# The last pair of a split-precision Strassen product: one product moved to the end, in two quarters

## The reference, cut to what matters

```python
# x: (8, 256, 1024) float32, 2048 tokens
base = einsum('btd,od->bto', x, W)                 # W: (1024, 1024)
logits = einsum('btd,ed->bte', x, Wr) + bias       # 8 experts, 5.0 added to the language's own
gates = softmax of the top 2 logits, 0 elsewhere
h = einsum('btd,erd->bter', x, A)                  # rank 16
y = base + 2.0 * einsum('bter,bte,eor->bto', h, gates, B)
dots = softmax(y @ centroids.T / 0.1)              # 64 clusters
hits = dots > 0.01
query_sel, cluster_sel = any(hits, axis=1), any(hits, axis=0)
dense = y @ weight.T + ffn_bias                    # (1024, 1024)
out = x + where(query_sel[:, None] & cluster_sel[assignments][None, :], dense, 0)
```

## Time and profile before

| | us |
|---|---|
| median of 3 runs | 349.85 (349.26 to 349.99) |
| the profiled execution | 350.19 |
| its span, from the first to the last instruction | 348.1 |
| TensorE busy / weight loads | 337.4 / 296.7 |
| VectorE busy | 254.1 |
| ScalarE busy | 134.0 |
| granted TensorE clock, mean | 0.994 |

### The profile page before, as it was taken

One profiled execution on the slowest core, in us unless ns is written; L12 is line 12 of the kernel. 1 busy time (PEld: TensorE's weight loads), 2 busy tenths in 40 slices (PEclk: granted clock), 3 DMA queues, 4 the chain that ended last, 5 costly groups with the idle time before them and its releaser, 6 DMA issues.

```text
span 348.1 us, 4828 instructions
## 1 busy us (share of the span) xinstructions
PE 337.4 (97%) x1892; PEld 296.7 (85%) x1892; DVE 254.1 (73%) x439; ACT 134.0 (39%) x215; POOL 1.0 (0%) x9
## 2 busy tenths in 40 slices
PE   6799999999999999999999999999999999999993
PEld 6588888999999999999887888888888888888882
DVE  2627669557787787788976979849498494984926
ACT  4616464334564555645452422333223332233120
POOL 1000000000000000000000000000000000000000
PEclk9999999999999999999999999999999999999997
DMA  7576440345334333333813162733707336060303
GB/s 270 188 274 265 154 183 16 105 124 180 118 100 148 122 121 122 124 119 122 316 47 122 60 225 79 247 115 123 240 1 247 117 124 237 2 241 0 122 0 121
DMA packets 13782, 49.10 MB, mean 141 GB/s; under 512 B 1664, under 2 KB 1664, under 8 KB 13760
## 3 DMA queue, kind: packets, MB, share of 16 engines
q1 hardware_dynamic: 13760, 48.80, 40.1%
HBM read 40.41 MB, written 8.39 MB: 140 GB/s over the span
## 4 chain that ended last, share of the span: by engine, by line
PE 94%; DMA 2%; DVE 2%; issue 1%; ACT 0%; SPq 0%; DVEq 0%
PE ps L925 31%; PE ps L926 31%; PE ps L927 31%; DMA vt_raw<-in_v 2%; PE ps L985 1%; DVE u L838 0%; DVE vt_lo L580 0%; ACT vt_hi L393 0%; DVE u L902 0%; DVE u L814 0%; DVE nat L908 0%; DVE u L583 0%; ACT u L393 0%; PE ps L1047 0%; SPq L307 0%
## 5 line engine op out<-in xcount | busy, mean ns | idle before, releaser
L925 PE MATMUL ps<-vt_hi,w_hi 128*128 128x288 f32 (+1 forms) x216 | 71.4, 330 | 3.1 <-DVE vt_lo L580 3.1
L926 PE MATMUL ps<-vt_lo,w_hi 128*128 128x288 f32 (+1 forms) x216 | 70.4, 326 | 0.0
L927 PE MATMUL ps<-vt_hi,w_lo 128*128 128x288 f32 (+1 forms) x216 | 70.4, 326 | 0.0
L393 ACT ACTIVATE u<-ps 128x512 f32<-128x512 f32 x32 | 19.1, 598 | 88.5 <-PE ps L927 59.0
L926 PE MATMUL ps<-gop_lo,sl_s_hi 128*128 128x512 f32 x128 | 49.8, 389 | 0.0
L925 PEld LDWEIGHTS ps<-vt_hi,w_hi 128*128 128x128 f32 x216 | 40.6, 188 | 6.6 <-DVE vt_lo L580 2.4
L926 PEld LDWEIGHTS ps<-vt_lo,w_hi 128*128 128x128 f32 x216 | 40.6, 188 | 2.8
L927 PEld LDWEIGHTS ps<-vt_hi,w_lo 128*128 128x128 f32 x216 | 40.5, 188 | 2.8
L925 PE MATMUL ps<-gop_hi_t,sl_s_hi 128*128 128x512 f32 x96 | 37.5, 390 | 0.0
L927 PE MATMUL ps<-gop_hi_t,sl_s_lo 128*128 128x512 f32 x96 | 37.4, 389 | 0.0
L925 PE MATMUL ps<-aw_hi,xt_hi 128*128 128x200 f32 x128 | 35.5, 278 | 0.1
(11 more groups left out here) (123 smaller groups left out, 637.3 us busy)
## 6 DMA issues: line engine op xcount, KB each, us to landing
xt_raw<-in_xt SPq DMA_DIRECT2D x32, 512.0 KB, 4.0
nat<-in_x SPq DMA_DIRECT2D x16, 512.0 KB, 4.3
out<-nat SPq DMA_DIRECT2D x15, 512.0 KB, 2.7
wraw<-in_w SPq DMA_DIRECT2D x9, 512.0 KB, 3.4
w_raw<-in_w SPq DMA_DIRECT2D x8, 512.0 KB, 3.3
vt_raw<-in_v SPq DMA_DIRECT2D x4, 576.0 KB, 4.5
vt_raw<-in_v SPq DMA_DIRECT2D x4, 512.0 KB, 7.3
awt_raw<-in_awt SPq DMA_DIRECT2D x1, 544.0 KB, 6.0
```

Source lines behind the costliest of these rows:

```text
L393: return nc.scalar.activation(dst, src, ACT.Copy)
L925: nc.tensor.matmul(dst, l_hi, r_hi, start=start, stop=False, skip_group_check=True)
L926: nc.tensor.matmul(dst, l_hi, r_lo, start=False, stop=False, skip_group_check=True)
L927: return nc.tensor.matmul(dst, l_lo, r_hi, start=False, stop=stop, skip_group_check=True)
```

## The change

In the last pair (i = 7) alone:

- TensorE: l12 by R21 with its LoRA part is no longer second, but last. It is done in two quarters of 256 output columns: 15 matmuls of 256 columns into bank Y of the odd pairs, and 15 into bank Y of the even pairs. The matmuls of pair 7 become 81 of 512 columns and 30 of 256, instead of 96 of 512. Each weight of that product is loaded twice.
- VectorE, block 11: `add11(7)` is gone. Row 0 of `u`, as ScalarE left it (p1_kept), is masked and added to `nat` at once. Once block 12 is finished, each quarter of bank Y is multiplied by `qsel` and `mask_row` from PSUM, and added to `nat`: four instructions of 256 elements for each partition.
- VectorE, the end of pair 6, which stands in iteration 7: tile (6, 0) comes before tile (6, 1), and the split of pair 7's sums (`rest_s`) between them.
- SyncE: tile (7, 0) is stored as its second half and two quarters, each when `result[0]` has gone one further.

The core of the diff:

```diff
@@ SyncE
-            sp.wait_ge(result[0], i + 1)
-            at = slice(2 * i * P, (2 * i + 1) * P)
-            sp.dma_start(out_t[at, 0:HALF], nat[i % 2][0][:, 0:HALF]).then_inc(out_stored[i % 2][0], 16)
-            sp.wait_ge(result[0], i + 2)
-            sp.dma_start(out_t[at, HALF:FO], nat[i % 2][0][:, HALF:FO]).then_inc(out_stored[i % 2][0], 16)
+            parts = [slice(HALF, FO), slice(0, QUARTER), slice(QUARTER, HALF)]
+            for n, cols in enumerate(parts):
+                sp.wait_ge(result[0], i + 2 + n)
+                sp.dma_start(out_t[2 * i * P:(2 * i + 1) * P, cols],
+                             nat[i % 2][0][:, cols]).then_inc(out_stored[i % 2][0], 16)
...
@@ VectorE
+                elif i == NPAIR - 1:
+                    add22(i - 1)
+                    add21(i - 1)
+                    base(i - 1, 0)
+                    add12(i - 1)
+                    mask(i - 1, 0)
+                    finish(i - 1, 0)
+                    rest_s(i)
+                    base(i - 1, 1)
+                    mask(i - 1, 1)
+                    finish(i - 1, 1)
...
+            def masked_to(dst, src, cols):
+                return nc.vector.scalar_tensor_tensor(out=dst, in0=src, scalar=q0, in1=mask_row[:, cols],
+                                                      op0=ALU.mult, op1=ALU.mult)
...
             base(i, 0)
-            mask_last(0, f1, sum11)
+            dve.wait_ge(p1_kept, i + 1)
+            masked_to(u[:, 0, :], u[:, 0, :], f1).then_inc(masked[0], 1)
             base(i, 1)
-            finish_last(0, f1)
+            dve.wait_ge(masked[0], i + 1)
+            dve.wait_ge(based[0], i + 1)
+            nc.vector.tensor_tensor(at[:, f1], u[:, 0, :], at[:, f1], ALU.add).then_inc(result[0], 1)
             add22(i)
             add21(i)
             mask(i, 1)
             finish(i, 1)
             add12(i)
...
+            for h in range(2):
+                cols = slice(h * QUARTER, (h + 1) * QUARTER)
+                dve.wait_ge(y_bank, i + 1 + h)
+                masked_to(u[:, 0, cols], bank(i + h, BANK_Y)[:, cols], cols).then_inc(masked[0], 1)
+                dve.wait_ge(masked[0], i + 3 + h)
+                nc.vector.tensor_tensor(at[:, cols], u[:, 0, cols], at[:, cols], ALU.add).then_inc(result[0], 1)
...
@@ TensorE, behind the loop, which now ends with pair 6
+            for h in range(2):
+                cols = slice(h * QUARTER, (h + 1) * QUARTER)
+                dst = ps[:, 4 * ((i + h) % 2) + BANK_Y, cols]
+                pe.wait_ge(sum11, i - 1 + h)
+                for k in range(KH):
+                    l_hi, l_lo = l12(k)
+                    three(dst, l_hi, l_lo, gop_hi_r[:, R21, k, cols], gop_lo[:, R21, k, cols], k == 0, False)
+                t = slice(0, P)
+                three(dst, hgm_hi[i % 2][:, t], hgm_lo[i % 2][:, t], gb3_hi[:, 0, cols], gb3_lo[:, 0, cols], False,
+                      True).then_inc(y_bank, 1)
```

More of the change, by code:

```diff
@@ L16 @@
 HALF = 512
+QUARTER = HALF // 2
 LANG_BIAS = 5.0
@@ L360, in _ @@
             store(i, 1)
-            sp.wait_ge(result[0], i + 1)
-            at = slice(2 * i * P, (2 * i + 1) * P)
-            sp.dma_start(out_t[at, 0:HALF], nat[i % 2][0][:, 0:HALF]).then_inc(out_stored[i % 2][0], 16)
-            sp.wait_ge(result[0], i + 2)
-            sp.dma_start(out_t[at, HALF:FO], nat[i % 2][0][:, HALF:FO]).then_inc(out_stored[i % 2][0], 16)
+            parts = [slice(HALF, FO), slice(0, QUARTER), slice(QUARTER, HALF)]
[3 more added lines that the diff above has]
+                             nat[i % 2][0][:, cols]).then_inc(out_stored[i % 2][0], 16)
             for s in range(2):
                 for c in range(2):
-                    sp.wait_ge(out_stored[s][c], 16 * (NPAIR // 2 + (s == i % 2 and c == 0)))
+                    sp.wait_ge(out_stored[s][c], 16 * (NPAIR // 2 + (2 if s == i % 2 and c == 0 else 0)))
         @block.gpsimd
@@ L889, in _ @@
                     s_sums(i + 1)
-                add11(i)
-                if i + 1 < NPAIR:
+                    add11(i)
                     rest_a(i + 1)
@@ L898, in _ @@
             at = nat[i % 2][0]
[L900 to L908, removed]
+            q0 = qsel[:, 2 * i:2 * i + 1]
+            def masked_to(dst, src, cols):
+                return nc.vector.scalar_tensor_tensor(out=dst, in0=src, scalar=q0, in1=mask_row[:, cols],
+                                                      op0=ALU.mult, op1=ALU.mult)
             base(i, 0)
-            mask_last(0, f1, sum11)
+            dve.wait_ge(p1_kept, i + 1)
+            masked_to(u[:, 0, :], u[:, 0, :], f1).then_inc(masked[0], 1)
             base(i, 1)
-            finish_last(0, f1)
+            dve.wait_ge(masked[0], i + 1)
+            dve.wait_ge(based[0], i + 1)
+            nc.vector.tensor_tensor(at[:, f1], u[:, 0, :], at[:, f1], ALU.add).then_inc(result[0], 1)
             add22(i)
@@ L918, in _ @@
             add12(i)
-            mask_last(1, f2, sum12)
-            finish_last(1, f2)
+            dve.wait_ge(sum12, i + 1)
+            masked_to(u[:, 1, :], u[:, 1, :], f2).then_inc(masked[0], 1)
+            dve.wait_ge(masked[0], i + 2)
+            nc.vector.tensor_tensor(at[:, f2], u[:, 1, :], at[:, f2], ALU.add).then_inc(result[0], 1)
+            dve.wait_ge(result[0], i + 1)
+            for h in range(2):
[4 more added lines that the diff above has]
+                nc.vector.tensor_tensor(at[:, cols], u[:, 0, cols], at[:, cols], ALU.add).then_inc(result[0], 1)
         @block.tensor
@@ L1056, in lora21 @@
                 lora(i, BANK_V, 1, 2).then_inc(v_bank, 1)
-            for i in range(NPAIR):
+            for i in range(NPAIR - 1):
                 pe.wait_ge(sa_split, i + 1)
@@ L1104, in _ @@
                     column_mask()
+            i = NPAIR - 1
+            pe.wait_ge(sa_split, i + 1)
+            pe.wait_ge(sum22, i - 1)
+            product(i, BANK_X, l11, R11, True).then_inc(x_bank, 1)
+            pe.wait_ge(s22_split, i + 1)
+            pe.wait_ge(sum21, i - 1)
+            product(i, BANK_V, l22, T4, True, False)
+            pe.wait_ge(hgm_split, i + 1)
+            lora21(i)
+            pe.wait_ge(ss_split, i + 1)
+            pe.wait_ge(p1_kept, i + 1)
+            product(i, BANK_X, s_of(S2), T2, False).then_inc(x_bank, 1)
+            pe.wait_ge(sum12, i - 1)
+            product(i, BANK_W, s_of(S1), T1, True).then_inc(w_bank, 1)
+            pe.wait_ge(u2_kept, i + 1)
+            product(i, BANK_X, s_of(S3), T3, False, False)
+            lora(i, BANK_X, 1, 1).then_inc(x_bank, 1)
+            pe.wait_ge(p5_kept, i + 1)
+            product(i, BANK_W, s_of(S4), R22, False, False)
+            lora(i, BANK_W, 0, 1).then_inc(w_bank, 1)
+            for h in range(2):
[8 more added lines that the diff above has]
+                      True).then_inc(y_bank, 1)
 _INS = ["x", "xt", "itok_B_0_7", "w9", "awt", "v1", "v2", "L0_ffn_bias", "L0_ffn_assignments"]
```

## The result

| | us, median | lowest to highest | ratio to before, 95% interval |
|---|---|---|---|
| before, 4 runs | 349.77 | 349.26 to 349.99 | |
| after, 4 runs | 346.97 | 346.65 to 347.08 | 0.9923 [0.9907, 0.9938] |
| after, 10 runs later (after_again), before 349.66 | 347.55 | 346.85 to 350.03 | 0.9942 [0.9909, 0.9975] |
| after, 12 runs later still (after_third), before 349.43 | 348.02 | 346.93 to 349.97 | 0.9949 [0.9924, 0.9975] |

The change makes the kernel faster. The two later ones, with more runs, gave 2.1 and 1.4 us by their medians. The rest of the first 2.8 they put down to the first 12 us of the program, which the change doesn't touch.

What follows compares the result with a forecast made beforehand. TensorE was taken to bound the kernel until its last product, with VectorE's queue setting the end. VectorE's -1.66 and the store's -0.2 gave -1.86 us, from 349.85 to 348.0, range 347.3 to 348.9.

Steps and rivals of the forecast that it cites:

- Part 1: TensorE in pair 7: moving l12 by R21 last brings everything behind it, and VectorE's add22, 3.40 us earlier.
- Part 2: VectorE's tail: seven unchanged instructions, then four new ones of 256 elements; its end moves from 345.46 to 343.80, -1.66 us.
- Part 3: TensorE's last 30 matmuls: 0.1195 us a step, ending at 342.34, hidden by 0.5 us before VectorE asks at 342.85.
- Rivals 2 and 3: TensorE's short matmuls: loads never overlapping, 349.6 us, chance 0.03; or each load waiting for the matmul ahead, 352.8, 0.03.
- Part 4: End of pair 6: VectorE's new order ends the split at 325.93, in time for TensorE at 326.34; cost 0, bounds 0 to 0.5.
- Rival 1: TensorE at 326.3: the split comes too late and TensorE stops, costing 0.1 to 0.5 us; 348.3 us, chance 0.15.
- Part 5: Last store: 128 KB instead of 256 KB lands in 1.9 us (bounds 1.8 and 2.1) instead of 2.1, -0.2 us.
- Rival 4: Last stores: the new ones get in each other's way, the last landing after 3.0 us; 349.1 us, chance 0.05.
- The rule on PSUM: VectorE's two multiplies from PSUM: by the rule 0.13 us more, sum -1.73; the forecast took no extra cost.

Runs made afterwards that it cites:

- after_again: The changed kernel run again with no edit, 10 runs: 347.55 us, ratio 0.9942 to before.
- after_third: The changed kernel run once more with no edit, 12 runs: 348.02 us, ratio 0.9949 to before.
- late_split: The changed kernel with VectorE's order at the end of pair 6 put back as it was before: 351.1 us, ratio 1.0039 to before.
- one_piece: The changed kernel with the last product in one piece of 512 columns and the tile stored as two halves: 348.16 us, ratio 0.9961 to before.
- before_again: The kernel before the change, run again with no edit: 349.66 us, ratio 0.9997 to before.

## Why the prediction was wrong, and where it was right

Measured from pair 7's first matmul, the steps came out as follows.

- **Part 1, right.** add22 was to start at 336.08 - 320.22 = 15.86 us and started at 334.79 - 318.93 = 15.86.
- **Part 2, right.** The multiply of 256 elements was taken as 0.49 and took 0.47 and 0.48; the adds took 0.42. VectorE's end was to be at 343.80 - 320.22 = 23.58 and was at 23.54. The line through the two rows of the same instruction was the right choice between the bounds.
- **Part 3, right.** 29 steps from 337.29 to 340.76 are 0.1197 us each, 0.1195 were taken; TensorE ended at 341.04, 0.50 us ahead of the second multiply. Rivals 2 and 3, with steps of 0.19 and 0.30, fall with it.
- **Part 4, right.** The split was to end at 5.71 us and ended at 324.67 - 318.93 = 5.74. TensorE did not stop: its first matmul that needs the split stood at 325.05, 0.38 us behind the split's end. The cover is thin, and late_split shows its price. Rival 1 falls, for this order.
- **Part 5, a little too small.** The last store landed after 1.7 us, 1.9 were taken, with 1.8 as the lower bound. With the rest of the end, 0.31 us were gained for 0.2. Rival 4 falls. By the rule of the Trainium skill, "DMA: Bandwidth & Descriptors", section "Anatomy of one DMA", whose fit is for GpSimd's path, the estimate was 2.3 us; the trace, with stores from SyncE's queue, disagrees.
- **The rule on PSUM.** A multiply of 512 elements from PSUM took 0.75 in one_piece and one from SBUF 0.75 before. The Trainium skill, "VectorE: DVE Perf Modes", section "The TRN2 errata", has 120 fixed cycles for a source in PSUM and 58 for SBUF; no run here shows a difference.

The sum of the tail is -2.01 us where -1.86 stood. The step that failed is the last one of the sum, which carried it from the profiled execution to the median: "the same sum gives 349.85 - 1.86". It held all that lies ahead of pair 7 for equal in all executions, and took the spread from three runs that lay within 0.73 us. The runs showed in its place that the unchanged kernels begin their second group between 10.05 and 11.54 us, and pair 7 between 318.84 and 321.96. The range failed with that step: with 0.6 taken off its own lower bound, 347.7, it would have begun at 347.1 and not at 347.3, and 346.97 lies below that too. The trace of before did show TensorE without work for 1.12 us ahead of its first group and for 2.01 ahead of its second, in the first 12 us; the prediction left them aside, since the change doesn't touch them. The 114 executions of before in the four larger sets lie from 348.54 to 351.97, 15 of them above 351.4; of the changed kernel's 26, 6 lie above 349.7. The four first executions of the changed kernel all fell into its fastest part, 346.65 to 347.08; with 22 more the ratio is 0.9942 and 0.9949, which for a median of 349.8 would be 347.8 to 348.0.

That this was luck and not the program is shown for the starts: after_again and after_third have the late one, before_again the early one. That the remaining 0.8 us of the first comparison are that and nothing else is inferred from the table: the first four executions of the changed kernel left one profile, and it has an early start. Whether late starts are equally frequent in all the kernels is open. So is why one or two parts of a load land some 1.6 us behind the others in one execution and not in another.

## What to carry to other kernels

Where a matrix engine bounds a kernel, ask which of its products the chain behind it needs first and which one output alone needs; moved to the end, that last one runs while the other engine works on what came before it (here 3.40 us off VectorE's start, of which the four new instructions took 1.70). The products that now come sooner need their operands sooner: bring those forward as well, and count the margin. In late_split, without that, the same move cost more than it brought.

A prediction of some tenths of a per cent needs the spread of the kernel's start as well as the sum. Compare stretches that begin at a common instruction, not spans.

## What the runs showed of the hardware

The same program began its work on two schedules, with its second group near 10.05 or 11.5 us, depending on when the last parts of the first loads landed. A stop of TensorE of some 2 us at 9.5 to 11.5 us cost itself alone in the profile of before, and in after_again another 1.6, since the granted clock fell behind it. In the profile of before (1.12 and 2.01 us without work) it did not fall and in after_again (1.35 and 2.06) it did. In after_third it fell at about 8 us, behind a stop of 1.96 us ahead of the first group, and before_again had 1.83 in the same place and kept it. So the rows here don't tell these apart by the length of the stop.

A store of 128 KB landed after 1.7 us, one of 256 KB after 2.0 or 2.1, but after 3.0 where it was issued 0.4 us behind one of 512 KB.
